# Gated self-attention over 512 keys: where the softmax sums are formed, who adds the exponentials, and when they are inverted

## What is computed

```python
q = einsum('bsc,hcd->bhsd', xn, wq)
k = einsum('btc,hcd->bhtd', yn, wk)
v = einsum('btc,hcd->bhtd', yn, wv)
a = softmax(einsum('bhsd,bhtd->bhst', q, k) * D ** (-0.5), axis=-1)
mask = (arange(t)[None, :] > arange(s)[:, None])   # keys after the query only
a = a * mask                                        # after the softmax
o = einsum('bhst,bhtd->bhsd', a, v)
x_out = x + concat_heads(o) @ li1_w + li1_b
```

## Time and profile before

| what | value |
|---|---|
| median of 3 runs | 1875.61 us |
| lowest and highest of them | 1861.08, 1893.85 us |
| the profiled execution: its time | 1872.87 us |
| its span, first to last instruction | 1871.1 us |
| granted TensorE clock, mean over the span | 0.877 |
| TensorE matmuls busy | 1605.9 us (86%) |
| VectorE busy | 844.2 us (45%) |
| ScalarE busy | 720.7 us (39%) |
| GpSimd busy | 147.0 us (8%) |

### The profile page before, as it was taken

The page is one execution under the profiler, slowest core; times in us unless marked ns, Lnnn a source line. Parts: engine busy times, 40 slices in busy tenths (PEclk is TensorE's granted clock), DMA queues, the critical chain, the costliest instruction groups (busy, mean ns, idle before and its releaser), DMA issues.

```text
span 1871.1 us, 22418 instructions
## 1 busy us (share of the span) xinstructions
PE 1605.9 (86%) x9052; PEld 741.8 (40%) x9052; DVE 844.2 (45%) x1666; ACT 720.7 (39%) x1267; POOL 147.0 (8%) x207
## 2 busy tenths in 40 slices
PE   5948999979899989987659999798999989888387
PEld 2322333332344435733324322342444436543284
DVE  4283564253456343234555662342564442437312
ACT  2334455323545225242344554433454134242033
POOL 0000111100012000000000112000021000002321
PEclk9568899999999688997778999999898789889688
DMA  4000000000000100000000000000000100021241
GB/s 184 1 0 1 1 1 1 1 1 1 0 1 1 46 1 1 1 1 2 1 1 1 1 1 1 0 1 1 0 2 1 46 1 1 1 70 10 67 138 59
DMA packets 18107, 30.17 MB, mean 16 GB/s; under 512 B 4640, under 2 KB 12640, under 8 KB 17104
## 3 DMA queue, kind: packets, MB, share of 16 engines
q1 hardware_dynamic: 16752, 26.10, 4.3%
q0 software_dynamic: 1248, 2.59, 0.4%
HBM read 23.49 MB, written 5.19 MB: 15 GB/s over the span
## 4 chain that ended last, share of the span: by engine, by line
PE 78%; DVE 11%; ACT 6%; issue 2%; DMA 1%; SPq 1%; POOL 0%; POOLq 0%; DVEq 0%; ACTq 0%
PE ps L817 7%; PE ps L920 5%; PE ps L682 4%; PE ps L853 3%; PE ps L627 3%; PE ps L1358 3%; PE ps L1370 3%; PE ps L1058 3%; PE ps L721 3%; PE ps L1050 3%; PE ps L971 3%; PE ps L951 2%; PE ps L867 2%; PE ps L842 2%; PE ps L659 2%
## 5 line engine op out<-in xcount | busy, mean ns | idle before, releaser
L2039 DVE TENSOR_REDUCE peak<-ps 128x1 f32<-128x512 f32 x256 | 163.9, 685 | 129.1 <-PE ps L817 129.0
L1658 ACT ACTIVATE big<-ps 128x512 f32<-128x512 f32 x256 | 140.0, 595 | 135.2 <-PE ps L844 127.7
L842 PE MATMUL ps<-qT,pp 32*128 32x512 f32 x512 | 162.1, 659 | 0.0
L817 PE MATMUL ps<-pp,qT 32*128 32x512 f32 x512 | 149.3, 672 | 2.0 <-ACT pp L1762 1.4
L1679 ACT ACTIVATE big<-ps 128x512 f32<-128x512 f32 (+3 forms) x256 | 101.2, 437 | 116.8 <-PE ps L951 115.9
L2078 DVE TENSOR_REDUCE crest<-ps 128x2 f32<-128x512 f32 (+3 forms) x128 | 105.2, 824 | 66.5 <-PE ps L926 66.3
L951 PE MATMUL ps<-qT,pp 32*128 32x384 f32 (+3 forms) x512 | 130.8, 521 | 2.3 <-ACT big L1679 1.4
L1612 ACT ACTIVATE big<-ps 77x1024 f32<-77x1024 f32 x96 | 93.4, 1016 | 86.6 <-PE ps L682 86.2
L1966 DVE TENSOR_REDUCE small<-ps 128x8 f32<-128x616 f32 x96 | 74.3, 797 | 91.0 <-PE ps L655 53.6
L920 PE MATMUL ps<-pp,qT 32*128 32x384 f32 (+3 forms) x512 | 110.3, 500 | 4.6 <-DVE crest L2078 2.3
L1592 ACT ACTIVATE sq<-ps 128x512 f32<-128x512 f32 x48 | 28.7, 597 | 197.4 <-PE ps L627 197.4
(11 more groups left out here) (480 smaller groups left out, 2733.6 us busy)
## 6 DMA issues: line engine op xcount, KB each, us to landing
...
```

The source lines that it names most:

```text
L817: pe.matmul(rbank(x), qT[at, u, k, 128 * i:128 * i + 128], keyT(u, k)[at, :], start=True, stop=True, tile_position=(32 * c, 0)).then_inc(* ...
L842: pe.matmul(tbank(y), keyT(u, k)[at, 128 * j:128 * j + 128], qT[at, u, k, :], start=True, stop=False, tile_position=(32 * c, 0))
L1658: A(prob(m)[:, TURN_OF[g], :], tbank(tplace(m, g)), ACT.Exp).then_inc(*SCALAR.did("a1", "exp", m, g))
L2039: v.tensor_reduce(peak[:, p // 4 % 2, i, c:c + 1], rbank(ring(p, c)), AX.X, ALU.max)\
```

## The change

What it does:

- GpSimd adds the exponentials of each pair of key tiles, head by head (four `tensor_tensor` of 128 x 512 float32 for each pair, `both`), each as soon as ScalarE's exponential of the second tile is there, and then masks the two tiles. `both` is a single buffer, so the next pair waits for TensorE's sums of this one.
- `sums` runs once for each pair, at the end of even iterations, on `both`, with a matrix of ones in all 32 rows. The bank holds one quad's sums after two pairs, and ScalarE copies it out every four iterations.
- `values` comes one iteration later (m - 3), so the loop has 35 iterations, and ScalarE's copy of a quad's result moves by one.
- VectorE inverts each quad's sums in four pieces of 128 columns, one after each `maxima(p)` from p = 11, and multiplies the quad's result after the fourth (both operands in SBUF). Quads 6 and 7 are inverted whole after the loop.
- The 32 spreading matmuls are gone. The projection of slot 0 (`joined(0)`) is issued at m = 32 before the last sums, that of slot 1 after the loop, head by head. Both use banks 2 and 3.

```diff
--- before.py
+++ after.py
@@ -361,6 +361,7 @@
 
         vt1 = pt[:].rearrange("p a b -> p (a b)")[:, 0:2048].rearrange("p (j f) -> p j f", j=4)
 
+        both = pt[:].rearrange("p a b -> p (a b)")[:, 2048:4096].rearrange("p (c s) -> p c s", c=4)
         shift = spare[:, 0:512].bitcast(BF16).rearrange("p (a s) -> p a s", a=2)
         cut = spare[:, 512:768].bitcast(BF16).rearrange("p (i c r) -> p i c r", i=4, c=4)
 
@@ -549,12 +550,20 @@
                 pool.sem_inc(turn_begins, 1)
 
             def keep():
-                for n in range(32):
-                    j = ktile_of(n)
-                    diag = prob(n)[:, :, 128 * j:128 * j + 128]
-                    pool.wait_ge(*TENSOR["a1", "den", n])
-                    pool.affine_select(diag, diag, pattern=[[0, 4], [-1, 128]], compare_op=ALU.is_gt, fill=0.0,
-                                       base=0, channel_multiplier=1).then_inc(*POOL.did("a1", "mask", n))
+
+                for last in range(1, 32, 2):
+                    if last > 1:
+                        pool.wait_ge(*TENSOR["a1", "den", last - 2])
+                    for g, c in enumerate(TURN_OF):
+                        pool.wait_ge(*SCALAR["a1", "exp", last, g])
+                        pool.tensor_tensor(both[:, c, :], prob(last - 1)[:, c, :], prob(last)[:, c, :], ALU.add)\
+                            .then_inc(*POOL.did("a1", "both", last, g))
+                    pool.wait_ge(*POOL["a1", "both", last, 3])
+                    for n in (last - 1, last):
+                        j = ktile_of(n)
+                        diag = prob(n)[:, :, 128 * j:128 * j + 128]
+                        pool.affine_select(diag, diag, pattern=[[0, 4], [-1, 128]], compare_op=ALU.is_gt, fill=0.0,
+                                           base=0, channel_multiplier=1).then_inc(*POOL.did("a1", "mask", n))
 
             def columns_of_ones():
 
@@ -795,7 +804,7 @@
                                            stop=True, tile_position=(0, 32 * c))
                         mm.then_inc(*TENSOR.did(tag, "spread", u, k))
 
-            def attend(project):
+            def attend(project, joined):
 
 
 
@@ -845,14 +854,13 @@
                               stop=True, tile_position=(32 * c, 0)).then_inc(*TENSOR.did("a1", "T", n, g))
 
                 def sums(n):
-                    k = n // 4 % 4
-                    pe.wait_ge(*SCALAR["a1", "exp", n, 3])
-                    if n == 16:
-                        pe.wait_ge(*SCALAR["a1", "den", 0])
+
+                    pe.wait_ge(*POOL["a1", "both", n, 3])
+                    if n % 4 == 1 and n > 1:
+                        pe.wait_ge(*SCALAR["a1", "den", n // 4 - 1])
                     for c in range(4):
-                        mm = pe.matmul(PSB[1][32 * c:32 * c + 32, :],
-                                       K["col8"][:, 128 * k + 32 * c:128 * k + 32 * c + 32], prob(n)[:, c, :],
-                                       start=n % 16 == 0, stop=n % 16 == 15, tile_position=(0, 32 * c),
+                        mm = pe.matmul(PSB[1][32 * c:32 * c + 32, :], K["ones"][:, 0:32], both[:, c, :],
+                                       start=n % 4 == 1, stop=n % 4 == 3, tile_position=(0, 32 * c),
                                        skip_group_check=True)
                     mm.then_inc(*TENSOR.did("a1", "den", n))
 
@@ -875,30 +883,22 @@
                 turned(0)
                 for c in range(4):
                     rowscore(5, c)
-                for m in range(34):
+                for m in range(35):
                     if m % 4 == 3 and m < 28:
                         turned((m + 1) // 4)
                     for g in range(4):
-                        if g == 2 and m >= 2:
-                            values(m - 2)
+                        if g == 2 and m >= 3:
+                            values(m - 3)
                         if m + 6 < 32:
                             rowscore(m + 6, g)
                         if m < 32:
                             colscore(m, g)
-                    if 1 <= m < 33:
+                    if m == 32:
+                        pe.wait_ge(*VECTOR["a1", "max", 31, 3])
+                        joined(0)
+                    if m % 2 == 0 and 2 <= m < 33:
                         sums(m - 1)
-                for u in U:
-                    pe.wait_ge(*VECTOR["a1", "inv", u])
-                    for k in range(4):
-                        at = 4 * u + k
-                        if at >= 6:
-                            pe.wait_ge(*VECTOR["a1", "O", 0, at - 6])
-                        for c in range(4):
-                            row = 32 * c + 8 * k
-                            mm = pe.matmul(PSB[2 + at % 6][32 * c:32 * c + 32, :],
-                                           K["ident"][:, row:row + 1].to_broadcast([128, 32]), rs[:, u, :], start=True,
-                                           stop=True, tile_position=(0, 32 * c))
-                        mm.then_inc(*TENSOR.did("a1", "spread", u, k))
+                joined(1)
 
             def attend_past(token_values, logits):
 
@@ -1196,8 +1196,16 @@
                                            (xn if kind == "q" else x2)[:, u, :], start=True, stop=True)
                         mm.then_inc(*TENSOR.did("a1 made", n))
 
-                attend(project)
-                reduce4("a1 li1", w["a1_li1"], lambda u: qT[:, u, :, :], lambda u: [SCALAR["a1", "o", 7], VECTOR["a1", "O", u, 3]])
+
+                def joined(u):
+
+                    for c in range(4):
+                        pe.wait_ge(*VECTOR["a1", "O", u, c])
+                        mm = pe.matmul(PSB[2 + u], w["a1_li1"][:, 128 * c:128 * c + 128], qT[:, u, c, :], start=c == 0,
+                                       stop=c == 3)
+                    mm.then_inc(*TENSOR.did("a1 li1", u))
+
+                attend(project, joined)
                 norm("a1n3", lambda u: x2[:, u, :], lambda u: VECTOR["a1 x2", u])
                 mlp("a1m", w["a1_li2"], w["a1_li3"])
                 context_kv("a2", w["a2_wk"], w["a2_wv"], cn, 32)
@@ -1656,14 +1664,16 @@
                             if m >= 4 and g == 0:
                                 act.wait_ge(*TENSOR["a1", "AV", m - 4])
                             A(prob(m)[:, TURN_OF[g], :], tbank(tplace(m, g)), ACT.Exp).then_inc(*SCALAR.did("a1", "exp", m, g))
-                    if m >= 5 and m % 4 == 1:
-                        Q = (m - 5) // 4
+                    if m >= 6 and m % 4 == 2:
+                        Q = (m - 6) // 4
                         act.wait_ge(*TENSOR["a1", "AV", 4 * Q + 3])
                         A(qT[:, Q // 4, Q % 4, :], PSB[0], ACT.Identity).then_inc(*SCALAR.did("a1", "o", Q))
-                    if m == 16 or m == 32:
-                        u = m // 16 - 1
+                    if m >= 4 and m % 4 == 0:
+                        Q = m // 4 - 1
                         act.wait_ge(*TENSOR["a1", "den", m - 1])
-                        A(sq[:, u, :], PSB[1], ACT.Identity).then_inc(*SCALAR.did("a1", "den", u))
+                        if Q >= 2:
+                            act.wait_ge(*VECTOR["a1", "inv", Q - 2])
+                        A(sq[:, Q % 2, :], PSB[1], ACT.Identity).then_inc(*SCALAR.did("a1", "den", Q))
 
             def attend_past():
                 for u in U:
@@ -2029,7 +2039,7 @@
                         v.tensor_tensor(qT[:, u, k, :], qT[:, u, k, :], PSB[2 + (4 * u + k) % 6], ALU.mult)\
                             .then_inc(*VECTOR.did(tag, "O", u, k))
 
-            def attend():
+            def attend(residual_of):
                 def maxima(p):
                     i = p % 4
                     for c in range(4):
@@ -2048,23 +2058,29 @@
                     v.tensor_tensor(cut[:, :, :, 2 * k + 1], peak[:, Q % 2], cut[:, :, :, 2 * k], ALU.subtract)\
                         .then_inc(*VECTOR.did("a1", "cut", Q))
 
-                def inverse(u):
-                    v.wait_ge(*SCALAR["a1", "den", u])
-                    v.reciprocal(rs[:, u, :], sq[:, u, :]).then_inc(*VECTOR.did("a1", "inv", u))
+                def inverse(Q, lo, hi):
+
+                    v.wait_ge(*SCALAR["a1", "den", Q])
+                    ins = v.reciprocal(rs[:, Q % 2, lo:hi], sq[:, Q % 2, lo:hi])
+                    if hi == S:
+                        ins.then_inc(*VECTOR.did("a1", "inv", Q))
+                        own = qT[:, Q // 4, Q % 4, :]
+                        v.wait_ge(*VECTOR["a1", "inv", Q])
+                        v.wait_ge(*SCALAR["a1", "o", Q])
+                        v.tensor_tensor(own, own, rs[:, Q % 2, :], ALU.mult).then_inc(*VECTOR.did("a1", "O", Q // 4, Q % 4))
 
                 for p in range(32):
                     maxima(p)
                     if p % 4 == 3:
                         cut_off(p // 4)
-                    if p == 24:
-                        inverse(0)
-                inverse(1)
-                for u in U:
-                    for k in range(4):
```

(20 more changed lines are left out.)

## The result

The changed kernel takes 1899.85 us, median of 20 runs, where the kernel before takes 1861.14 in as many: it is slower. The quotient of these medians is 1.0208. The forecast was 1859 us, range 1838 to 1884, and a gain. The profiled execution of the changed kernel took 1888.56 us (span 1886.8), 15.7 more than the one of before.

The account below looks back on a forecast made before the run. TensorE was taken as bound by groups spaced at least 2.03 us by VectorE's and ScalarE's freeing of banks. Terms summed to -6.9 us a turn, two turns -13.8, from 1872.9 to 1859 us; range 1838 to 1884.

Parts of the forecast that it names:

- The bound: TensorE's loop: two groups cannot follow closer than 2.03 us, so of 1.98 us of sums a round about 0.9 returns.
- the stall of 0.38 us: TensorE's delay in a round, waiting for a bank; it was to go because staggered groups free banks earlier: -0.38 us.
- Reciprocals: VectorE's pieces between maxima, 0.95 us per 128 columns; with product and cut, lateness of +1.0 us a round.
- Adds: GpSimd's adds of exponentials, 1.25 us each: hidden behind half a round, with 0.5 to 1.0 us to spare.
- Contention: VectorE's subtraction of the cut waits for the rest of a GpSimd add: 0.6 us a round, bounds 0 and 1.25.
- Rival B: Cast and subtraction of the cut each wait behind another add: +15 us, 1874 us; chance 0.13.
- The end: From the last group to the norm: 12.0 us instead of 19.35, so -7.4 us a turn, bounds -5 and -8.
- the -0.7 of iterations 26 to 31: Iterations without row scores: two sets of sums gone, 0.3 to 0.4 us each, -0.7 us a turn.
- if the clock of 1.00 drops in the loop: One of three signs given at the prediction's end that would show it wrong; no size given.
- A: Maxima keep their rhythm, pieces and cut hide wholly: 8.4 us a turn gained, 1842 us; chance 0.15.
- C: GpSimd's adds bound the loop, TensorE waiting for `both` at each pair: 1889 us; chance 0.12.
- D: The product of result and inverse meets adds too, 0.8 us more in ten rounds: 1867 us; within the forecast's 0.60.

Follow-up runs that it names:

- half_sums: Changed kernel without GpSimd's adds, TensorE summing only the odd key tile of each pair (half of each softmax sum left out): 1858.90 us, ratio 0.9947.
- thin_pieces: Changed kernel with each reciprocal piece in the loop cut from 128 to 16 columns: 1872.79 us, ratio 1.0012.
- fill_thin: Changed kernel with four zero-weight matmuls ending each odd iteration from 3 on, and reciprocal pieces of 16 columns: 1879.91 us, ratio 0.9939 from 3 of 10 runs.
- fill_end: Changed kernel with four zero-weight matmuls at the end of iterations 27, 29 and 31 only: 1907.28 us, ratio 1.0213.

## Why the prediction was wrong

*The bound.* That two groups cannot follow closer than 2.03 us held: half_sums won back 0.47 of 1.98 us a round. Forecast were 0.9 and bounds from 0.5: the direction was right, the stall of 0.38 us that I had go did not show as a gain.

*Reciprocals.* 128 columns were put at 0.95 us and took 0.943. Their cost, with the product, was put at 1.0 us a round; the pieces are 0.70 by thin_pieces and fill_thin, and 0.24 with products and all where sums stand at every boundary.

*Adds.* Put at 1.25 us, measured 1.265, and hidden as forecast as long as there are row scores; in the end the sums wait 0.25 us for one.

*Contention.* Put at 0.6 us a round, measured 0.98 in the thin kernel (18.59 against half_sums' 17.61) and 0.59 to 0.65 in the dense ones. The subtraction waits for a whole add, 1.219 us as its median, not for the average rest of one. The reason is in the timeline of VectorE and GpSimd in the changed kernel:

```profile
209.36 2.49 POOL L559 TENSOR_TENSOR pt<-big 128x512 f32<-128x512 f32 x2
209.49 1.22 DVE L2058 TENSOR_TENSOR spare<-peak,spare 128x16 bf16<-128x16 f32 x1
...
210.59 0.94 DVE L2064 RECIPROCAL rs<-sq 128x128 f32<-128x128 f32 x1
...
211.46 2.52 DVE L2049 TENSOR_REDUCE peak<-ps 128x1 f32<-128x512 f32 x4
...
212.13 0.69 PE L826 MATMUL ps<-pp,qT 32*128 32x512 f32 x1 [0.49 <-DVE peak L2049]
...
213.41 1.64 PE L862 MATMUL ps<-pt,cst 128*32 128x512 f32 x8
...
215.52 1.22 PE L826 MATMUL ps<-pp,qT 32*128 32x512 f32 x1
```

The first section says that the engines wait for each other only through semaphores; here they do not. The cast meets an add and ends 0.06 us after that add does; by then the next add has begun (209.36), and the subtraction, which starts at 209.49 behind the cast, ends 0.09 us after the end of that one. It is so for all 14 casts and all 14 subtractions of this profile that meet adds; the first of each turn meets none and takes 0.20 and 0.23 us. So the cast sets the subtraction at the start of an add, and that is why it pays a whole one. The Trainium skill, SBUF — State Buffer, "Who interferes with whom", has the ports that the two engines share as an exclusive lock, which the one that issues first holds for its whole instruction while the other is blocked; the trace agrees, for the cast too. Rival B, both operations held up, is thus true as a mechanism, but not its price: the cast mostly starts 0.27 us before an add's end and loses 0.13 us (median 0.332 us; 0.761 and 1.050 at the second cut of each turn) and not a second whole add.

These errors cancel: 18.59 us measured, 18.6 forecast. From the runs the sum goes 17.84, +0.24 for pieces and products on a dense TensorE (18.08), -0.47 for the sums (17.61), +0.98 for the adds (18.59); the forecast had +1.0, -0.9 and +0.6. It was luck, and shows how little a right sum proves of its terms.

*The end.* The end of the tables begins at the last row score, so the forecast for it is -7.4 and the -0.7 of iterations 26 to 31, -8.1 us a turn; with filling, at full clock, it is 46.8 to 40.9 or 40.1, -5.9 to -6.7. Counted as in the forecast, from the end of the last group (and of the filling behind it) to the norm's second product, fill_end's first turn, all at full clock, takes 12.75 us (334.04 to 346.79) where 12.0 were forecast and 19.35 stand before: -6.6. In the changed kernel itself (all engines, first turn):

```profile
344.50 4.87 PE L1204 MATMUL ps<-qT,w_l 128*128 128x512 f32 x8
...
349.30 1.06 PE L862 MATMUL ps<-pt,cst 128*32 128x512 f32 x8
...
351.06 3.35 DVE L2064 RECIPROCAL rs<-sq 128x512 f32<-128x512 f32 x1 [0.90 <-ACT sq L1676]
...
354.44 1.19 DVE L2070 TENSOR_TENSOR qT<-qT,rs 128x512 f32<-128x512 f32 x1
...
355.69 1.13 PE L1204 MATMUL ps<-qT,w_l 128*128 128x512 f32 x2 [1.90 <-DVE qT L2070]
```

The order is the forecast one: slot 0's projection ahead of the last sums, the reciprocal, the product, the last matmul. It is stretched by the clock: slot 0's four matmuls of `li1` take 4.87 us, in fill_end's first turn 3.70, and the eight of before 7.13. The last product takes 1.19 us and not the 0.75 of the forecast: GpSimd is in a copy (L574) when it starts, and it ends 0.54 us after that copy. Here an operation of VectorE with two inputs in SBUF meets GpSimd on the path, in both turns.

**The step that failed** is one that has no line of its own in the sum: every price was taken from a loop whose clock was 1.00, so that the clock's share was put at nothing without a reason, and I wrote only at the end that I would be wrong "if the clock of 1.00 drops in the loop". It does, and at the loop's end for longer. The same timeline shows it begin: after the pieces and the cut TensorE stands idle for 0.49 us for VectorE's maximum, and the sums at 213.41 take 1.64 us instead of 1.06, the groups behind them at 1.22 instead of 0.69 a matmul. A turn has 10 to 17 us more at 0.5 in its loop and 28 at its end. The end shows the price: 50.6 us with 28 us at 0.5, 40.9 without, so 0.35 us lost for each us at the low clock. So the turn is 14.2 and 11.5 us longer where 6.9 less were forecast. Of the 21.1 us missed in the first turn, 9.7 are the clock's in the end, about 6 its in the loop (17.1 us at that price, an estimate), 2.2 the end at full clock (-5.9, with the filling in it, for -8.1), and some 3 are left in the loop. Part of these is at its start, where the forecast had a gain of 0.9 us and TensorE stood idle for 1.08 us at 190.89, behind the first cut that met adds.

None of the rivals was this one. A had the loop faster, B and C had VectorE and GpSimd as the cause, and C's ground, TensorE waiting for `both`, is not seen in the rounds at full clock. D, the product meeting the adds, did not come: its median is 0.692 us, near the 0.7 that it was put at, and only the last product of a turn met GpSimd, in a copy. The other side of the forecast was reached by another way than any I had priced.

What is not settled: which part of the falls within the loop is due to VectorE's pieces and which to the cut, since taking away either removed them; why the first turn of the changed kernel has 6.8 us more of it than the second; whether it is the missing matmuls or the idle moments of 0.25 to 0.67 us that let the clock fall at the end, since the filling removes both; and how often it falls there in executions without a profile.
